# A two-layer graph network: where the folded weights are stored, where W1 is loaded, and two groups of unused products

## The chip, the cores and the metric

The kernel runs as one launch on one core of a Trainium2 chip. The metric is the device time of one execution in microseconds (us). Before the change it is 2430.15 us, the median of three runs (2429.15 to 2435.55).

A core has five engines with a queue each: TensorE (PE, matmuls; PEld is its weight load), VectorE (DVE), ScalarE (ACT), GpSimd (POOL) and SyncE (SP, which here does nothing but issue transfers). They run side by side and wait for each other by semaphores. In the profile an fp32 matmul shows as two records.

## The reference

`x` holds 1,250 nodes of 512 values. There are 40,000 edges (`src`, `dst`) with 8 values each. All matrices are fp32.

```python
xn = layernorm(x)
x = x + gnn0(xn, edges, edge_attr) + mix0(xn)       # graph attention with its feed-forward; linear attention
x = x + ffn0(layernorm(x))                          # causal attention and a soft mixture of 8 experts
xn = layernorm(x)
x = x + gnn1(xn, edges) + mix1(xn)                  # normalised sum over neighbours; additive attention
x = x + ffn1(layernorm(x))                          # product-key lookup, 16 of 8192 experts for each of 8 heads

def gnn0(x, src, dst, bias):                        # the part around the first edits
    z = layernorm(x) * g + b
    q, k, v = z @ Wq.T + bq, z @ Wk.T + bk, z @ Wv.T + bv           # 8 heads of 64
    s = sum(q[src] * k[dst]) / 8 + bias
    p = exp(s - segment_max(s, src)[src])
    alpha = p / segment_sum(p, src)[src]
    x = x + segment_sum(alpha * v[dst], src) @ Wo.T + bo
    z = layernorm(x) * g2 + b2
    return x + silu(z @ W1.T + b1) @ W2.T + b2

def gnn1(x, src, dst):                              # W_gcn @ W_dense is what the kernel folds
    h = (x @ W_gcn)
    agg = segment_sum(h[src] * norm, dst) + b_gcn   # with self loops
    return agg @ W_dense + b_dense
```

The lookup at the very end takes, for each node and head, the 16 best pairs of keys, and adds up the up-projections of their experts with softmax weights. In the kernel this comes out as one weight for each of 256 experts and a matmul with 256 rows of `weight_up_embed`.

## The kernel before

The 1,250 nodes are ten tiles of 125 rows (`TILES`, `TP`). The program is written by hand as one list of instructions for each engine; a stage is a group of functions of one name (`gnn_*`, `att_*`, `ff_*`, ..., `last_*`), and each engine runs its functions in the order of the blocks at the end of the file. Nothing reorders them, so an instruction stands behind everything that is written ahead of it on its engine.

GpSimd first scatters the edges into a dense table in device memory, one row of nine values for each pair of nodes: eight summed attention factors and the count of edges (`edge_table`, filled up when `table_filled` is passed). The graph attention then runs over this table in `BLOCKS` = 50 blocks: five chunks `c` of 250 source nodes, each with ten tiles `b` of 125 target nodes. A block of the table is 125 x 2250 fp32. It is loaded by `load_block(i)` in two pieces of 112 and 13 rows (helper `spread`, lines 211 and 212) into a ring of three buffers (`RING` = 3). Block i+3 is issued on SP when block i's four products are made (`a_p`) and behind the store of block i's counts (`a_cc`), so the ring is always two blocks ahead.

A block has four steps n, a pair of heads each. TensorE makes the scores of step n+2 (lines 1313 and 1316) and adds up the values of step n (line 1326); ScalarE takes the exponential in place (line 1290); VectorE multiplies with the factors from the table (line 1231) and releases both the values of step n and the scores of step n+2; GpSimd adds up the denominators (line 1263). Once in a block ScalarE gathers the counts (line 1278), TensorE transposes them (line 1338), ScalarE copies them (line 1295) and SP stores them in `adjacency`. From the second chunk on, the denominators and the output projection of the chunk before stand between the steps (lines 1349, 1361, 197).

Ahead of the first step the attention has a piece that belongs to a later stage: `fold_dense_pe` multiplies W_gcn by W_dense and folds the two biases (lines 1567, 1568, 1560), and `fold_dense_act` copies the result into the arena (lines 1578 to 1583), which is `f_step` 5. SP stores it in device memory (`wgd`, `l1_bias`, line 1182 and 1183). Its place in the arena is then used for three quarters of the feed-forward's W1 (`w1_most`), so W1's load waits for the store (`s_fold`); the last quarter is `w1_last`. The feed-forward waits for W1, W2 and its biases by `s_wf`. The stored weights are read back several stages later.

The lookup (`last_*`) works tile by tile. For the last tile VectorE masks the pairs (line 2803, two halves) and spreads the rest (line 2566), TensorE turns both into a bank by matmuls with the identity (`weights(t)`: lines 2946 and 2950, eight each), VectorE weighs them (line 2773), TensorE multiplies by `up_p` (`out(t)`, through `project`, line 197), VectorE adds the result to x (line 2777), and SP stores it. `out(t-1)` stands ahead of `weights(t)` on TensorE.

## Time and profile before

| | |
|---|---|
| median of three runs | 2430.15 us (2429.15 to 2435.55) |
| the profiled execution | 2428.97 us |
| its span in the profile | 2427.2 us |
| mean granted clock of TensorE | 0.939 of 2.4 GHz |
| busy: PE, DVE, ACT, POOL | 89%, 54%, 30%, 34% |
| chain that ended last: PE, DVE, POOL, ACT, issue, DMA | 62%, 15%, 10%, 5%, 5%, 3% |
| 780 to 820 us: PE busy, clock, DMA share | 25.3 of 40 us, 0.74, 0.93 |

The profile shows one execution: for each engine its busy time, and for each idle time of an engine the instruction or transfer that ended it. The chain is followed back from the last instruction, at each step to what released it. Granted clock is the share of 2.4 GHz that TensorE was given in a stretch; it has two levels, 1.00 (2.4 GHz) and 0.50 (1.2 GHz). DMA share is the mean busy share of the 16 DMA engines. Times in the rows below are from the start of the span.

### The profile page before, as it was taken

Reading aid. Unit: us, or ns where it says so; the run is one execution under the profiler, and the core shown is the slowest. Engines: PE = TensorE matmul, PEld = TensorE weight load, DVE = VectorE, ACT = ScalarE, POOL = GpSimd, SP = SyncE. Lnnn points to the kernel's source line nnn. Section 1 sums busy time; section 2 is a strip of 40 time slices with the busy share of each in tenths; the row PEclk is TensorE's granted clock in tenths of the full one; section 3 lists DMA queues with packets and bytes.
Section 4 is the critical chain, followed back from the end, with each engine's and each line's share of the span. In section 5 each row is a group of like instructions: output and inputs, shape, how many; then the busy total and the mean of one; then the engine's idle time right before and its main releaser. Section 6 shows DMA issues by size and latency. Waiting matters only on the chain.

```text
span 2427.2 us, 31743 instructions
## 1 busy us (share of the span) xinstructions
PE 2166.4 (89%) x11604; PEld 1264.2 (52%) x11604; DVE 1320.5 (54%) x4053; ACT 732.4 (30%) x1620; POOL 832.8 (34%) x648
## 2 busy tenths in 40 slices
PE   3999976899797899998899999998999998989975
PEld 2455544444332444444676447666866664455553
DVE  4555577577994566665222553343022225259997
ACT  4111111222001444443222335555411111034452
POOL 2018888788786655665000000000000000013442
PEclk9998877899898899999999998999999999999986
DMA  9992222222323867765300002000300005000000
GB/s 362 419 361 3 3 3 3 4 4 4 55 3 41 235 167 184 186 170 143 118 1 10 1 19 87 1 1 24 116 1 1 1 1 127 16 1 9 10 10 18
DMA packets 87071, 177.28 MB, mean 73 GB/s; under 512 B 64674, under 2 KB 65661, under 8 KB 70812
## 3 DMA queue, kind: packets, MB, share of 16 engines
q1 hardware_dynamic: 41169, 173.38, 22.1%
q0 software_dynamic: 45072, 1.46, 5.8%
q8 instruction: 93, 1.52, 0.3%
q14 instruction: 63, 0.52, 0.1%
q10 hardware_dynamic: 674, 0.39, 0.1%
HBM read 106.88 MB, written 68.31 MB: 72 GB/s over the span
## 4 chain that ended last, share of the span: by engine, by line
PE 62%; DVE 15%; POOL 10%; ACT 5%; issue 5%; DMA 3%; SPq 0%; DVEq 0%; ACTq 0%; POOLq 0%
PE banks L197 18%; POOL edge_table L537 7%; PE banks L2131 6%; PE banks L2171 6%; PE banks L1495 3%; PE banks L1313 3%; PE banks L354 2%; PE banks L1326 2%; PE banks L191 2%; PE banks L1967 2%; DMA edge_table<-arena 2%; PE banks L1940 2%; PE banks L1954 2%; POOL arena L1263 2%; PE banks L2553 2%
## 5 line engine op out<-in xcount | busy, mean ns | idle before, releaser
L197 PE MATMUL banks<-arena 128*125 128x512 f32 x1200 | 561.3, 615 | 17.6 <-DVE arena L2773 15.2
L537 POOL DMA_INDIRECT edge_table<-arena x313 | 489.0, 1562 | 241.4 <-DMA edge_table<-arena 147.1
L197 PEld LDWEIGHTS banks<-arena 128*125 128x125 f32 x1200 | 223.5, 194 | 293.1 <-issue 267.3
L1231 DVE TENSOR_TENSOR arena<-banks,arena 125x500 f32<-125x500 f32 x200 | 208.5, 1052 | 143.0 <-ACT banks L1290 106.0
L1263 POOL TENSOR_TENSOR arena<-arena 125x500 f32<-125x500 f32 x180 | 222.5, 1246 | 141.0 <-DVE arena L1231 135.3
L2580 POOL CAST arena<-arena 125x128 f32<-125x128 uint32 x10 | 2.9, 290 | 719.2 <-DVE arena L2716 719.2
L1313 PE MATMUL banks<-arena 64*125 64x250 f32 x800 | 141.7, 432 | 35.8 <-DVE arena L1231 29.4
L2079 DVE SCALAR_TENSOR_TENSOR arena<-banks,arena 125x512 f32<-125x512 f32 x80 | 60.1, 751 | 189.4 <-PE banks L2171 189.4
L1290 ACT ACTIVATE banks<-banks 125x500 f32<-125x500 f32 x200 | 114.5, 573 | 159.6 <-PE banks L1316 159.2
L2131 PEld LDWEIGHTS banks<-arena 128*128 128x128 f32 x1280 | 144.0, 192 | 6.7 <-issue 6.6
L2131 PE MATMUL banks<-arena 128*128 128x125 f32 x1280 | 146.4, 276 | 0.1
L1834 DVE CUSTOM_DVE_ANT_0 arena<-banks,arena 125x512 f32<-125x512 f32 (+8 forms) x144 | 71.7, 552 | 134.0 <-PE banks L1940 130.7
L191 PE MATMUL banks<-arena 125*128 125x125 f32 x560 | 90.4, 298 | 56.2 <-DVE arena L185 37.7
L2171 PE MATMUL banks<-arena 128*125 128x512 f32 x320 | 139.2, 593 | 0.0
L1326 PE MATMUL banks<-arena 125*64 125x250 f32 x800 | 130.6, 405 | 0.9 <-ACT arena L1269 0.7
L191 PEld LDWEIGHTS banks<-arena 125*128 125x128 f32 x560 | 69.0, 153 | 115.4 <-issue 58.7
L363 ACT ACTIVATE arena<-banks 128x512 f32<-128x512 f32 x80 | 47.8, 598 | 252.3 <-PE banks L354 243.4
L1089 PE MATMUL banks<-arena 64*125 64x512 f32 (+1 forms) x480 | 113.1, 574 | 7.0 <-DVE arena L987 5.7
L1313 PEld LDWEIGHTS banks<-arena 64*125 64x125 f32 x800 | 60.8, 186 | 108.3 <-DVE arena L1231 65.7
L987 DVE TENSOR_REDUCE arena<-banks 125x2 f32<-125x1024 f32 (+1 forms) x120 | 112.0, 1010 | 0.0
L1800 POOL MEMSET arena<- 128x1250 f32 x1 | 1.1, 1140 | 308.8 <-ACTq L143 308.8
L2098 ACT ACTIVATE arena<-banks,arena 128x125 f32<-128x125 f32 x160 | 44.9, 367 | 203.4 <-PE banks L2131 203.4
(353 smaller groups left out, 3553.0 us busy)
## 6 DMA issues: line engine op xcount, KB each, us to landing
edge_table<-arena SPq DMA_DIRECT2D x24, 2250.0 KB, 37.0
arena<-edge_table SPq DMA_DIRECT2D x50, 984.4 KB
arena<-L_ffn_W SPq DMA_DIRECT2D x4, 2048.0 KB, 11.1
arena<-edge_table SPq DMA_DIRECT2D x50, 114.3 KB
adjacency<-arena SPq DMA_DIRECT2D x50, 109.4 KB
arena<-adjacency SPq DMA_DIRECT2D x10, 546.9 KB
edge_table<-arena POOLq DMA_INDIRECT x313
arena<-x SPq DMA_DIRECT2D x1, 2240.0 KB
```

The lines of the kernel that those rows point to most:

```text
L191: last = nc.tensor.transpose(dst[:, k, :], src[:, k * 128:(k + 1) * 128], ident[0:TP, 0:TP])
L197: last = nc.tensor.matmul(dst, xT[:, i, :], w[:, i, 0:n], start=(i == 0), stop=(i == k - 1))
L537: pool.indirect_dma_start(d["table"], bass.IndirectOffsetOnAxis(ap=cell[0:EP, c:c + 1].bitcast(U32), axis=0), vals[0:EP, c * ROW:(c + 1) * ...
L987: nc.vector.tensor_reduce(by_part_max[:, t, j, :, u % 3], both[:, :, 0:b - a], AX_X, ALU.max).then_inc(g_mx, 1)
L1089: last = nc.tensor.matmul(bank(2 * (u % 4) + e)[0:TP, 0:b - a], qT_g[64 * e:64 * e + 64, j, tok(t)], kT_g[64 * e:64 * e + 64, j, a:b], sta ...
L1231: nc.vector.tensor_tensor(P_g[n % PRING][0:TP, :].rearrange("p (e n) -> p e n", e=2), two_scores(n), ring[(c * TILES + b) % RING][0:TP, :, ...
L1263: nc.gpsimd.tensor_tensor(total_p, P_g[(n - PAIRS) % PRING][0:TP, :] if b == 1 else total_p, P_g[n % PRING][0:TP, :], ALU.add).then_inc(a_ ...
L1290: nc.scalar.activation(two_scores(n), two_scores(n), ACT.Exp).then_inc(a_e, 1)
L1313: nc.tensor.matmul(bank(at + e)[0:TP, 0:CHUNK], kT_g[64 * e:64 * e + 64, j, tok(b)], qT_g[64 * e:64 * e + 64, j, sources(c)], start=True, ...
L1326: last = nc.tensor.matmul(bank(j // 2)[64 * e:64 * e + 64, CHUNK * (j % 2):CHUNK * (j % 2 + 1)], V_g[0:TP, b, DH * (2 * j + e):DH * (2 * j ...
L2131: last = nc.tensor.matmul(bank(2 + n % 3)[:, m * TP:(m + 1) * TP], w1_e[a // 2][:, k, (c % 8) * 128:(c % 8 + 1) * 128], yT[:, k, tok(t)], ...
L2171: last = nc.tensor.matmul(bank(5 + n % 3)[0:TP, :], hT_e[t % 2][:, 2 * e + c, :], w2_e[e // 4][:, 2 * (e % 4) + c, :], start=(c == 0), sto ...
```

## The change

On SP, the store of the folded weights and bias and the two loads of W1 leave their place between `load_block(2)` and the loop over the blocks. They are issued inside the loop, at i = 10 (store), 20 (three quarters of W1) and 30 (the last quarter), each behind the load of block i+3. On TensorE, seven products of the identity with tiles of V are added behind the folding; they write bank 3, whose contents nobody reads before it is written anew. Seven more, of the identity with `up_p` into bank 0, are added for the last tile between `out(8)` and `weights(9)`; bank 0 is not read again. The results of these fourteen are not used. V, `up_p` and the identity are in place by then.

```diff
--- before.py
+++ after.py
@@ -1178,12 +1178,6 @@
 
             for i in range(RING):
                 load_block(i)
-            sp.wait_ge(f_step, 5)
-            sp.dma_start(d["wgd"], wgd_out.rearrange("p k n -> p (k n)")).then_inc(s_fold, 16)
-            sp.dma_start(d["l1_bias"], bias_out[0:1, :]).then_inc(s_fold, 16)
-            sp.wait_ge(s_fold, 32)
-            sp.dma_start(w1_most, d["L0_gnn_W1"][:, 0:3 * HID]).then_inc(s_wf, 16)
-            sp.dma_start(w1_last, d["L0_gnn_W1"][:, 3 * HID:4 * HID]).then_inc(s_wf, 16)
             for i in range(BLOCKS):
                 c, b = divmod(i, TILES)
                 sp.wait_ge(a_cc, i + 1)
@@ -1191,6 +1185,15 @@
                 if i + RING < BLOCKS:
                     sp.wait_ge(a_p, PAIRS * (i + 1))
                     load_block(i + RING)
+                if i == TILES:
+                    sp.wait_ge(f_step, 5)
+                    sp.dma_start(d["wgd"], wgd_out.rearrange("p k n -> p (k n)")).then_inc(s_fold, 16)
+                    sp.dma_start(d["l1_bias"], bias_out[0:1, :]).then_inc(s_fold, 16)
+                if i == 2 * TILES:
+                    sp.wait_ge(s_fold, 32)
+                    sp.dma_start(w1_most, d["L0_gnn_W1"][:, 0:3 * HID]).then_inc(s_wf, 16)
+                if i == 3 * TILES:
+                    sp.dma_start(w1_last, d["L0_gnn_W1"][:, 3 * HID:4 * HID]).then_inc(s_wf, 16)
             sp.wait_ge(a_s, ASTEPS)
             sp.dma_start(w2_g.rearrange("p k n -> p (k n)"), d["L0_gnn_W2"]).then_inc(s_wf, 16)
             for v in range(2):
@@ -1373,6 +1376,8 @@
             fold_dense_pe(pe)
             table_filled(pe)
             pe.wait_ge(f_step, 5)
+            for n in range(7):
+                nc.tensor.matmul(bank(3)[0:TP, :], ident[0:TP, 0:TP], V_g[0:TP, n, :], start=True, stop=True)
             for n in range(ASTEPS):
                 c, b, j = place(n)
                 m = n % PER
@@ -2976,6 +2981,9 @@
                 if t + 2 < TILES:
                     prepare(t + 2)
                     similarities(t + 2)
+                if t == TILES - 1:
+                    for n in range(7):
+                        nc.tensor.matmul(bank(0)[0:TP, :], ident[0:TP, 0:TP], up_p[0:TP, n % 2, :], start=True, stop=True)
                 weights(t)
             out(TILES - 1)
```

SP's queue at the start of the attention, before; 112x2250 and 13x2250 are the two pieces of a block, `gcn_dense_weights` is the store, 128x3072 and 128x1024 are W1:

```order
L211 DMA arena<-edge_table 112x2250
L212 DMA arena<-edge_table 13x2250
L1182 DMA gcn_dense_weights<-arena 128x2048 [waits fold_step]
L1183 DMA l_bias<-arena 1x512
L1185 DMA arena<-L_gnn_W 128x3072 [waits folded_weights_stored]
L1186 DMA arena<-L_gnn_W 128x1024
L211 DMA adjacency<-arena 112x2x125 [waits att_counts_copied]
L212 DMA adjacency<-arena 13x2x125
L211 DMA arena<-edge_table 112x2250 [waits att_weights_ready]
L212 DMA arena<-edge_table 13x2250
```

After, the same place, beginning with block 2:

```order
L211 DMA arena<-edge_table 112x2250
L212 DMA arena<-edge_table 13x2250
L211 DMA adjacency<-arena 112x2x125 [waits att_counts_copied]
L212 DMA adjacency<-arena 13x2x125
L211 DMA arena<-edge_table 112x2250 [waits att_weights_ready]
L212 DMA arena<-edge_table 13x2250
L211 DMA adjacency<-arena 112x2x125 [waits att_counts_copied]
L212 DMA adjacency<-arena 13x2x125
```

The four transfers between block 2 and the first counts are gone; the counts and the load of block 3 follow at once. The store stands here now, behind the load of block 13:

```order
L211 DMA adjacency<-arena 112x2x125 [waits att_counts_copied]
L212 DMA adjacency<-arena 13x2x125
L211 DMA arena<-edge_table 112x2250 [waits att_weights_ready]
L212 DMA arena<-edge_table 13x2250
L1190 DMA gcn_dense_weights<-arena 128x2048 [waits fold_step]
L1191 DMA l_bias<-arena 1x512
L211 DMA adjacency<-arena 112x2x125 [waits att_counts_copied]
L212 DMA adjacency<-arena 13x2x125
L211 DMA arena<-edge_table 112x2250 [waits att_weights_ready]
L212 DMA arena<-edge_table 13x2250
```

What moved is only the place in the queue; the number of transfers is the same.

TensorE behind the folding, before; lines 1567 to 1568 are the bias, 1560 the four parts of the product, 1313 the scores of step 2:

```order
L1560 MATMUL banks<-arena 128x512 x8
L1560 MATMUL banks<-arena 128x512 [waits fold_step]
L1560 MATMUL banks<-arena 128x512 x7
L1313 MATMUL banks<-arena 125x250 [waits fold_step,att_weights_ready,columns_scattered_1,columns_scattered_0]
L1313 MATMUL banks<-arena 125x250
L1316 MATMUL banks<-arena 125x250 x2
```

After, with lines shifted by a few; line 1380 is the new group:

```order
L1565 MATMUL banks<-arena 128x512 x8
L1565 MATMUL banks<-arena 128x512 [waits fold_step]
L1565 MATMUL banks<-arena 128x512 x7
L1380 MATMUL banks<-arena 125x512 [waits fold_step,columns_scattered_1,columns_scattered_0]
L1380 MATMUL banks<-arena 125x512 x6
L1316 MATMUL banks<-arena 125x250 [waits att_weights_ready]
L1316 MATMUL banks<-arena 125x250
L1319 MATMUL banks<-arena 125x250 x2
```

The seven products stand ahead of the scores of step 2 and have taken over their wait for the folding and for the filled table.

TensorE at the end of the program, before: transposes of tile 8, its output product, transposes and output product of tile 9:

```order
L197 MATMUL banks<-arena 125x512 [waits peer_weighted_gelu_ready]
L197 MATMUL banks<-arena 125x512
L2946 MATMUL banks<-arena 128x125 [waits peer_bank_step_of_act,peer_weights_masked]
L2946 MATMUL banks<-arena 128x125 x7
L2950 MATMUL banks<-arena 128x125 [waits peer_weights_masked]
L2950 MATMUL banks<-arena 128x125 x7
L197 MATMUL banks<-arena 125x512 [waits peer_weighted_gelu_ready]
L197 MATMUL banks<-arena 125x512
```

After:

```order
L197 MATMUL banks<-arena 125x512 [waits peer_weighted_gelu_ready]
L197 MATMUL banks<-arena 125x512
L2986 MATMUL banks<-arena 125x512 x7
L2951 MATMUL banks<-arena 128x125 [waits peer_bank_step_of_act,peer_weights_masked]
L2951 MATMUL banks<-arena 128x125 x7
L2955 MATMUL banks<-arena 128x125 [waits peer_weights_masked]
L2955 MATMUL banks<-arena 128x125 x7
L197 MATMUL banks<-arena 125x512 [waits peer_weighted_gelu_ready]
L197 MATMUL banks<-arena 125x512
```

The new group, line 2986, stands between the output product of tile 8 and the transposes of tile 9, and waits for nothing of its own.

## Rows read from the trace of the kernel before

**Rows 1.** Chain of waits, 776 to 872 us: start us, us, what.

```profile
800.54 10.64 DMA arena<-edge_table
```

**Rows 2.** SP's issues, 779 to 801 us: start us, us, issue.

```profile
779.24 0.33 SPq L211 DMA_DIRECT2D arena<-edge_table  x1
...
781.98 0.39 SPq L1182 DMA_DIRECT2D gcn_dense_weights<-arena  x1
...
797.51 0.35 SPq L1185 DMA_DIRECT2D arena<-L_gnn_W  x1
...
800.12 0.38 SPq L211 DMA_DIRECT2D arena<-edge_table  x1
```

**Rows 3.** VectorE in time, 786 to 827 us: start, us, instruction, [idle before].

```profile
786.38 1.99 DVE L1231 TENSOR_TENSOR arena<-banks,arena 125x500 f32<-125x500 f32 x2 [33.35 <-DMA arena<-edge_table]
...
812.50 2.00 DVE L1231 TENSOR_TENSOR arena<-banks,arena 125x500 f32<-125x500 f32 x2 [7.66 <-ACT banks L1290]
...
820.73 2.10 DVE L1231 TENSOR_TENSOR arena<-banks,arena 125x500 f32<-125x500 f32 x2 [1.68 <-ACT banks L1290]
...
826.53 2.11 DVE L1231 TENSOR_TENSOR arena<-banks,arena 125x500 f32<-125x500 f32 x2 [0.89 <-ACT banks L1290]
```

**Rows 4.** TensorE in order of time, the same columns.

```profile
787.57 1.20 PE L1313 MATMUL banks<-arena 64*125 64x250 f32 x4 [8.59 <-DVE arena L1231]
...
866.44 0.90 PE L1313 MATMUL banks<-arena 64*125 64x250 f32 x4 [1.56 <-DVE arena L1231]
...
938.46 0.69 PE L1313 MATMUL banks<-arena 64*125 64x250 f32 x4 [1.56 <-DVE arena L1231]
```

**Rows 5.** Stretches: us, busy of engines, granted clock, DMA share, GB/s.

```profile
779.70:787.40 7.70, 0.00 (x0) 0.00 (x0) 1.02 (x2) 0.74 (x2) 0.00 (x0) 0.61 0.95 250
787.40:791.70 4.30, 4.13 (x18) 2.10 (x20) 2.02 (x3) 0.89 (x2) 0.00 (x0) 0.50 1.01 237
```

**Rows 6.** DMA issues, 778 to 800 us: count, KB, us to landing.

```profile
arena<-edge_table SPq DMA_DIRECT2D x3, 984.4 KB
arena<-L_gnn_W SPq DMA_DIRECT2D x1, 1536.0 KB, 7.1
...
arena<-L_gnn_W SPq DMA_DIRECT2D x1, 512.0 KB, 8.3
...
adjacency<-arena SPq DMA_DIRECT2D x1, 109.4 KB
```

**Rows 7.** Stretches, columns as in Rows 5.

```profile
786.40:797.50 11.10, 9.81 (x60) 4.93 (x62) 7.00 (x7) 4.57 (x11) 2.24 (x2) 0.76 0.88 257
...
820.00:860.00 40.00, 38.94 (x292) 19.22 (x292) 28.88 (x28) 22.55 (x49) 30.01 (x25) 1.00 0.82 216
```

**Rows 8.** Line 1278 on ScalarE, 856 to 1150 us.

```profile
L1278 ACT ACTIVATE arena<-arena x39: 638/651/664, 860.3 to 1133.7; 125x250 f32<-125x250 f32 x39
```

**Rows 9.** ScalarE in order of time, its last copy of the folded weights.

```profile
779.02 0.60 ACT L1583 ACTIVATE arena<-banks 128x512 f32<-128x512 f32 x1 [1.86 <-PE banks L1560]
```

**Rows 10.** TensorE in order of time, 2299 us: ten products of line 2553.

```profile
2299.20 8.75 PE L2553 MATMUL banks<-arena 125*125 125x512 f32 x20
```

**Rows 11.** Chain of work that ended last, 883 to 955 us.

```profile
883.98 3.44 PE banks L197 x8
...
954.48 3.44 PE banks L197 x8
```

**Rows 12.** TensorE in order of time, 2320 us and the end.

```profile
2320.42 2.05 PE L2946 MATMUL banks<-arena 125*128 125x125 f32 x16 [0.72 <-POOL arena L2617]
...
2403.89 3.77 PE L197 MATMUL banks<-arena 128*125 128x512 f32 x4 [3.68 <-DVE arena L2773]
2415.31 3.78 PE L2946 MATMUL banks<-arena 125*128 125x125 f32 x16 [7.64 <-DVE arena L2803]
```

**Rows 13.** Chain of work that ended last, 2419 us.

```profile
2419.08 2.23 PE banks L2950 x16
```

**Rows 14.** Stretches of the end, columns as in Rows 5.

```profile
2415.30:2419.40 4.10, 4.09 (x19) 4.09 (x20) 1.21 (x1) 0.00 (x0) 0.00 (x0) 0.50 0.02 4
```


## The prediction

> **What bounds the kernel now.** I read three places, in the order in which the diff names them: the start of the graph attention (776 to 872 us), its chunks (870 to 1140 us) and the last 30 us. First view, the chain of waits. At the attention's start its longest piece is no computation: from 800.54 us the chain stands 10.64 us on a transfer from `edge_table` into the arena, the load of one block of the edge table [rows 1]. Second view, SP's queue, for why that load was late. SP issues blocks 0 to 2 from 779.24 us, the store of the folded weights at 781.98, then waits until that store has landed, and from 797.51 issues both parts of W1; block 3 leaves only at 800.12 [rows 2], behind 2,048 KB of weights [rows 6] that nobody needs before the feed-forward, behind all fifty blocks. Third view, VectorE, as a ruler: it makes the first product of block 0 at 786.38, of block 3 at 812.50, of block 4 at 820.73, of block 5 at 826.53 [rows 3]. The last step, 5.80 us, is the pace of a block when nothing is missing; TensorE is then 97% busy (38.94 of 40.00 us) [rows 7]. Fourth view, the granted clock. TensorE sat idle 8.59 us before 787.57 [rows 4], and the stretch behind it ran at 0.50, the 1.2 GHz level [rows 5]: four records of line 1313 take 1.20 us there and 0.69 us at the full 2.4 GHz [rows 4]. So the attention's start loses time twice, to a late block and to a low clock after each idle time.
>
> At the end TensorE is idle 3.68 us before the output product of tile 8, which takes 3.77 us, and 7.64 us before the transposes of the last tile, whose first half takes 3.78 us [rows 12]; the granted clock over them is 0.50 [rows 14]. The same half took 2.05 us at 2320.42 [rows 12].
>
> **The change, part by part.**
>
> *Store and W1 loads moved.* One store (128 x 2,048 fp32, 1,024 KB), one small bias row, and two loads (1,536 and 512 KB) [rows 6] leave their place in front of block 3 and go behind the loads of blocks 13, 23 and 33. The saving is bounded by the ruler. From block 0 to block 4 VectorE needs 820.73 - 786.38 = 34.35 us [rows 3]; at the steady pace it is 4 x 5.80 = 23.20. The difference is 11.15 us, of which 820.73 - 812.50 - 5.80 = 2.43 is block 3 run at the low clock, and 8.72 the late block with the slow start of block 0.
>
> Is block 3 in time? At the steady pace it is wanted at 786.38 + 3 x 5.80 = 803.8. It may be issued once block 0's four products are made, about 791 to 793. The queue then still holds blocks 1 and 2. A block is 984.4 KB for 112 of 125 rows, so 1,099 KB or 1.125 MB; its share of the count table 109.4 x 125/112 = 122 KB or 0.125 MB [rows 6]. Everything issued before W1 had landed by 797.51; taking off the store's 1.05 MB at the 257 GB/s of that stretch [rows 7], 4.1 us, blocks 0 to 2 end at 793.4. The counts and block 3 are 1.25 MB, 4.9 us at that rate. For the fixed part of a transfer, block 0 took 786.38 - 779.24 = 7.1 us from issue to use, 2.7 more than its 4.4 us of data. Block 3 is there at 793.4 + 4.9 + 2.7 = 801.0, 2.8 us early. At 216 GB/s, the lowest rate of a row here [rows 7], it takes 0.9 us more and is still early. Block 4 and after need 4.9 us of queue per 5.80, which the stretch of 820 to 860 shows working with no stall [rows 7]. I take the whole gap as gone.
>
> *The same bytes in their new place.* From 860.3 to 1133.7 there are 39 gathers, a block each 273.4/38 = 7.19 us [rows 8]. A load is issued two blocks, 14.4 us, before it is wanted. The worst insertion is 1,536 KB (1.57 MB, 6.1 us): its block and it hold the queue 11.0 us, the next block is issued at 7.2, ends at 11.0 + 4.9 + 2.7 = 18.6, and is wanted at 7.2 + 14.4 = 21.6. 3.0 us are left; with the store (4.1 us) 5.0, with the 512 KB (2.0 us) 7.1. Cost nothing; the ring of three blocks covers it. Without that cover each would cost what block 3's lateness costs now, 11.15 less some 2.1 for the slow start of block 0: 9.1 us. SP's new waits are for events long past, and nothing is queued behind them that could be late.
>
> *Seven unused products behind the folding.* They wait for ScalarE's last copy of the folded weights, which ends at 779.02 + 0.60 = 779.62 [rows 9]. They are fp32, 125x125 by 125x512, the form of line 2553: ten in 8.75 us [rows 10], so 6.1 us for seven at the full level. The level is full there: the 7.70 idle us from 779.70 have a mean of 0.61, so it fell only some 1.7 us into them (0.11/0.50 x 7.70) [rows 5]. So they end at 785.8. The next real step cannot start before 787.4, when the first product of block 0 is made. So they lie wholly in idle time, with 1.6 us to spare, and leave that much idle instead of 8.59. Their worth is the slow start, contained in the 11.15: 4.3 us at half speed [rows 5] are about 2.1 us. If they ran at half they would take 12.2 us and hold the chain 4.5 us.
>
> *Seven unused products before the last transposes.* TensorE ends the output product at 2403.89 + 3.77 = 2407.66 and is free until 2415.31 [rows 12]. After 2415.3 the clock stood at 0.50 for 4.1 us of work and then rose [rows 14]; counted from 2403.89 that is 2408.0, and so the seven take 6.1 + 0.2 and end at 2413.9. If the rise comes 1.4 us later they end at 2414.6. Both are before 2415.31. Then the two halves of the transposes take 2 x 2.05 = 4.1 us (both halves are 16 records of one form) instead of 2419.08 + 2.23 - 2415.31 = 6.00 [rows 12, 13]. Saving 1.9, all on the chain.
>
> **The sum.** 11.15 + 1.9 = 13.05 us off the profiled execution's 2428.97: 2415.9. (Its span is 2427.2, 1.8 less.) That execution is 1.2 us below the median of the runs, 2430.15; halfway between the two, 2416.5.
>
> **The short idle times.** TensorE idles 1.56 us at the start of four chunks. Before 866.44 the clock fell all the same (line 1313 takes 0.90 for its four, then more), before 938.46 and two like it, it did not (0.69) [rows 4]. From there to the chunk's output product it is 883.98 - 866.44 = 17.54 us with the fall and 954.48 - 938.46 = 16.02 without [rows 4, 11]: a fall costs 1.5. The change leaves two such idle times, 1.6 us at 785.8 and 0.6 to 1.4 at 2413.9. One in four is the price that I give each. The Trainium skill ("TensorE: Matmul & The Clock Gate", Why this matters for your kernels) warns only of idle gaps of more than about 3 us between bursts; by that rule neither would count, and rival A would have no chance. The trace disagrees once in four, and the measurement decides.
>
> **The rivals.**
>
> A, a remaining short idle time lowers the clock: 1.5 us lost in front or 1.9 at the end, 2418 to 2420. For it: the row at 866.44. Against it: three of four.
>
> B, block 3 is still late. If TensorE's faster start pulls the deadline forward and the queue, with store traffic of the counts between, gives 200 GB/s, block 3 comes at 793.4 + 1.4 for a later issue + 6.3 + 2.7 = 803.8, at the deadline; anything worse costs that wait and, if TensorE cools, 2.43 more. At 2.5 us late the front gains 6 and the sum is 2421 to 2422. Against it: rates of 237 and 257 with a full queue [rows 5, 7].
>
> C, slower: the insertions each stall the ring. The next block's data and its forerunners are 2.50 + 1.57 = 4.07 MB in 21.6 - 2.7 = 18.9 us, so it decides at 215 GB/s; below it the stall of block 3 is rebuilt at blocks 14, 24 and 34, at up to 9.1 us each, 27 in all: 2416.5 + 27 = 2444. From two such stalls on the change is a loss. Against it: 257 with the queue full; the 216 row has it 82% busy, so it is demand and not the limit.
>
> D, the 13 us are mostly given back behind the attention, by clock falls that land otherwise or a load that now arrives at a worse moment: 2424 to 2430. Nothing in the profile shows a load wanted at once after the attention other than W2, whose issue follows the last scores and so moves along.
>
> **How the numbers follow.** Forecast 0.66 (own range 2413.5 to 2419), A 0.16, B 0.09, D 0.05, C 0.04. A difference of 0.3%, 7.3 us, is about what measurement tells from none; faster means below 2422.9. A and nearly all of B lie there: faster 0.90, same 0.06 (D and a slice of B), slower 0.04. The range for 8 in 10 holds the forecast, A and a part of B, and below it the chance that the fall at 866 goes too: 2411.5 to 2423.
>
> **What would show it.** Right: block 3's load issued near 792 instead of 800; VectorE's first product of block 4 about 23 us after that of block 0; no DMA in the chain at the start but block 0; 14 records of unused products between 779.7 and 785.8 at 0.43 us each; clock 1.00 at 788; no idle time of ScalarE on `edge_table` at blocks 14, 24, 34; at the end, the two halves in 4.1 us, beginning when VectorE's second masked half is done and not later. Wrong: a wait on `edge_table` anywhere after block 0, unused records of 0.85 us, or last transposes that wait for the unused products.

## The result and the profile after

The changed kernel takes 2421.33 us, the median of seven runs (2413.46 to 2424.99), against 2430.41 for seven runs of the kernel before beside it (2429.15 to 2435.55): ratio 0.9952, 95% interval 0.9939 to 0.9966. With the later runs there are 19 of the changed kernel (median 2417.5, mean 2418.4) and 79 of the one before (median 2430.5, mean 2431.0). By all 79 the change is worth 12.6 us of mean, but 32 of them stand beside e5 to e8 and e12, where the changed kernel as it is wasn't run and the one before was quicker (means of 2429.6 and 2428.7). In the three sets that hold both, the means lie 11.3, 15.2 and 14.7 us apart, 13.6 weighted by the changed kernel's runs. The medians of the first set showed 9.

| | before | after |
|---|---|---|
| profiled execution, its span | 2428.97, 2427.2 us | 2422.49, 2420.7 us |
| mean granted clock | 0.939 | 0.943 |
| issue of block 0's load | 779.24 | 786.00 |
| issue of block 3's load, counted from that | 20.88 | 12.60 |
| VectorE's first product, block 0 to block 4 | 34.35 | 23.19 |
| last tile's transposes to VectorE's weights | 6.02 | 3.87 |

The lines of the file are shifted by the edits: 1234 is line 1231 of before, 1293 is 1290, 1316 is 1313, 2951 and 2955 are 2946 and 2950.

SP after the change (start, us, issue) answers to [rows 2]. Block 3's load follows block 0 by 12.6 us:

```profile
786.00 0.33 SPq L211 DMA_DIRECT2D arena<-edge_table  x1
...
798.60 0.35 SPq L211 DMA_DIRECT2D arena<-edge_table  x1
```

VectorE, the columns of [rows 3]. Blocks 0, 3 and 4 are shown. Every block comes 5.80 us behind the last, and after block 0 none waits for a transfer:

```profile
793.15 2.00 DVE L1234 TENSOR_TENSOR arena<-banks,arena 125x500 f32<-125x500 f32 x2 [34.48 <-DMA arena<-edge_table]
...
810.54 2.12 DVE L1234 TENSOR_TENSOR arena<-banks,arena 125x500 f32<-125x500 f32 x2 [0.89 <-ACT banks L1293]
...
816.34 2.10 DVE L1234 TENSOR_TENSOR arena<-banks,arena 125x500 f32<-125x500 f32 x2 [0.90 <-ACT banks L1293]
```

TensorE around the unused products in front and at the first chunk bound, the columns of [rows 4]. Two idle times of 1.26 and 1.99 us stand where 8.59 stood, and line 1316 takes 0.69 us at once. At 862.05 the clock fell after 1.56 us, as it did before:

```profile
785.97 6.27 PE L1380 MATMUL banks<-arena 125*125 125x512 f32 x14 [1.26 <-DMA edge_table<-arena]
794.24 0.69 PE L1316 MATMUL banks<-arena 64*125 64x250 f32 x4 [1.99 <-DVE arena L1234]
...
862.05 0.86 PE L1316 MATMUL banks<-arena 64*125 64x250 f32 x4 [1.56 <-DVE arena L1234]
```

TensorE at the end answers to [rows 12]. The seven products end 0.59 us before the masked pairs are there, and each half of the transposes takes 2 us:

```profile
2399.52 3.78 PE L197 MATMUL banks<-arena 128*125 128x512 f32 x4 [3.67 <-DVE arena L2778]
2403.09 7.25 PE L2986 MATMUL banks<-arena 125*125 125x512 f32 x14
2410.94 2.05 PE L2951 MATMUL banks<-arena 125*128 125x125 f32 x16 [0.59 <-DVE arena L2808]
2412.82 1.95 PE L2955 MATMUL banks<-arena 125*128 125x125 f32 x16
```

Stretches, the columns of [rows 5]. The granted clock is 1.00 in front, where it was 0.50, and over the transposes, where [rows 14] had 0.50:

```profile
785.90:792.30 6.40, 6.27 (x14) 2.55 (x14) 0.00 (x0) 0.00 (x0) 0.00 (x0) 1.00 0.85 208
...
794.20:798.50 4.30, 4.26 (x32) 2.19 (x32) 3.04 (x3) 2.29 (x6) 0.00 (x0) 1.00 1.04 251
...
2410.90:2414.90 4.00, 3.84 (x32) 3.65 (x32) 1.32 (x2) 0.00 (x0) 0.00 (x0) 1.00 0.01 2
```

The loads of W1 in their new place (DMA issues: count, KB, us to landing) landed in 11.3 and 7.6 us, and no engine waited for them or for a block behind them:

```profile
arena<-L_gnn_W SPq DMA_DIRECT2D x1, 1536.0 KB, 11.3
...
arena<-L_gnn_W SPq DMA_DIRECT2D x1, 512.0 KB, 7.6
```

Together: 11.16 us less from block 0 to block 4 and 2.15 less at the end are 13.3, but the span is only 6.5 shorter, because the first load left 6.8 us later, at 786.00 instead of 779.24. That point is ruled by GpSimd's scatter into the table. Its line in the views of 160 to 790 us (busy, mean ns, idle before and what ended it) is, before and after:

```profile
L537 POOL DMA_INDIRECT edge_table<-arena x313 | 489.0, 1562 | 241.4 <-DMA edge_table<-arena 147.1 <-issue 90.0 <-DVE arena L454 4.3
```

```profile
L537 POOL DMA_INDIRECT edge_table<-arena x313 | 490.9, 1568 | 246.1 <-DMA edge_table<-arena 147.3 <-issue 90.7 <-DVE arena L454 8.0
```

The two kernels have the same instructions there. Over the 14 profiles taken in all, the first load left between 774.26 and 786.60 us: from 776.03 to 781.73 in the three without products in front, over the whole of that range in the eleven with them. Fourteen profiles show no relation to the version; a small one they couldn't exclude. One profile of each kernel can't be compared by its span; the stretches can.

### The profile page after: what moved, and what is told of

Its sections match the earlier page's. It is cut to its first block, busy times and chain, and to the rows that moved or that the text cites. A ratio compares the mean times of both kernels' runs of the same rounds, so it can differ in the third digit from the quotient of the medians.

```text
span 2420.7 us, 31798 instructions
## 1 busy us (share of the span) xinstructions
PE 2180.0 (90%) x11632; PEld 1267.2 (52%) x11632; DVE 1320.2 (55%) x4053; ACT 732.3 (30%) x1620; POOL 834.7 (34%) x648
## 4 chain that ended last, share of the span: by engine, by line
PE 61%; DVE 15%; POOL 11%; ACT 5%; issue 5%; DMA 2%; DVEq 0%; SPq 0%; ACTq 0%; POOLq 0%
PE banks L197 17%; POOL edge_table L537 9%; PE banks L2136 6%; PE banks L2176 6%; PE banks L1500 3%; PE banks L1316 3%; PE banks L1329 2%; PE banks L191 2%; PE banks L1972 2%; PE banks L1945 2%; PE banks L1959 2%; PE banks L354 2%; POOL arena L1266 2%; PE banks L2558 2%; DMA edge_table<-arena 2%
## 5 line engine op out<-in xcount | busy, mean ns | idle before, releaser
L197 PE MATMUL banks<-arena 128*125 128x512 f32 x1200 | 568.3, 621 | 17.6 <-DVE arena L2778 15.2
L537 POOL DMA_INDIRECT edge_table<-arena x313 | 490.9, 1568 | 246.1 <-DMA edge_table<-arena 147.3
```

What stands on the lines that cost most here:

```text
L197: last = nc.tensor.matmul(dst, xT[:, i, :], w[:, i, 0:n], start=(i == 0), stop=(i == k - 1))
L537: pool.indirect_dma_start(d["table"], bass.IndirectOffsetOnAxis(ap=cell[0:EP, c:c + 1].bitcast(U32), axis=0), vals[0:EP, c * ROW:(c + 1) * ...
```

## The experiments

For each profile, in us: when block 0's load is issued; d, from there to the end of ScalarE's last copy of the folded weights (line 1583, 1588 after); VectorE's first product from block 0 to 1, and from block 0 to 4; from block 4 to the end of the span.

| kernel | load 0 | d | block 0 to 1 | 0 to 4 | 4 to end |
|---|---|---|---|---|---|
| before | 779.24 | +0.38 | 7.75 | 34.35 | 1606.47 |
| after | 786.00 | -0.65 | 5.79 | 23.19 | 1604.36 |
| e1_queue_only | 781.73 | +4.62 | 8.52 | 25.91 | 1603.34 |
| e2_front_only | 782.93 | +6.59 | 10.60 | 34.59 | 1607.18 |
| e3_end_only | 776.03 | -0.52 | 7.47 | 33.90 | 1600.70 |
| e4_whole_again | 784.31 | +2.36 | 6.14 | 23.56 | 1603.39 |
| e5_store_first | 780.66 | +2.16 | 6.36 | 23.76 | 1601.15 |
| e6_four_stores | 785.26 | +2.37 | 6.25 | 23.65 | 1603.45 |
| e7_three_products | 783.57 | +0.53 | 7.89 | 25.31 | 1605.19 |
| e8_twelve_products | 786.60 | +0.51 | 8.46 | 25.86 | 1609.37 |
| e9_more_places | 782.79 | +3.17 | 6.78 | 24.23 | 1596.77 |
| e10_seven_stores | 779.44 | +2.03 | 6.02 | 23.44 | 1609.83 |
| e11_whole_third | 779.78 | +4.57 | 8.42 | 25.86 | 1603.29 |
| e12_four_in_front | 774.26 | +2.31 | 5.79 | 23.19 | 1590.33 |

Each experiment is told by its difference from the changed kernel; `...` in a diff stands for lines left out.

**e1, the queue alone.** No unused products.

```diff
-            for n in range(7):
-                nc.tensor.matmul(bank(3)[0:TP, :], ident[0:TP, 0:TP], V_g[0:TP, n, :], start=True, stop=True)
...
-                    for n in range(7):
-                        nc.tensor.matmul(bank(0)[0:TP, :], ident[0:TP, 0:TP], up_p[0:TP, n % 2, :], start=True, stop=True)
```

> Only the moves in SP's queue, no unused products. Theory (two separate causes in front: a late block 3, and a low clock after the idle time): block 3's load is issued near 13 us after block 0's instead of 21, no wait on the edge table after block 0, but the first block still runs at the low clock. From VectorE's first product of block 0 to that of block 4: 23.2 us plus some 1.9 = 25.1 us (before 34.35, whole change 23.2). Time 2430.4 - 9.2 = 2421 if the stage ahead of the attention is as long as before. Rival 1 (the unused products do the work, the moved transfers nothing): 34 us and the time of before. Rival 2 (the change lengthens the 780 us ahead of the attention, where the changed kernel's profile stood 6.8 us later, through the moves on SP): block 0's load is issued near 786 us here too and the time is 2425.

2419.23 us (2414.57 to 2427.88, 12 runs) against 2432.84, ratio 0.9952 (0.9937 to 0.9968). The late block is gone. What stays is a slow block 0, 8.52 instead of 5.80. TensorE, in order of time:

```profile
790.24 1.20 PE L1316 MATMUL banks<-arena 64*125 64x250 f32 x4 [4.52 <-DVE arena L1234]
```

Idle for 4.52 us, then the lower level: 2.7 us. The queue's part of the 11.15 is thus 34.35 - 25.91 = 8.4 us.

**e2, the products in front alone.** Store and W1 loads back ahead of block 3, no products at the end.

```diff
+            sp.wait_ge(f_step, 5)
+            sp.dma_start(d["wgd"], wgd_out.rearrange("p k n -> p (k n)")).then_inc(s_fold, 16)
...
+            sp.dma_start(w1_last, d["L0_gnn_W1"][:, 3 * HID:4 * HID]).then_inc(s_wf, 16)
             for i in range(BLOCKS):
...
-                if i == TILES:
-                    sp.wait_ge(f_step, 5)
...
-                    for n in range(7):
-                        nc.tensor.matmul(bank(0)[0:TP, :], ident[0:TP, 0:TP], up_p[0:TP, n % 2, :], start=True, stop=True)
```

> Only the seven unused products behind the folding; the store and W1's loads stand where they stood before. Theory: block 0 starts at the full clock and is 1.9 us shorter, but block 3's load is still issued behind W1 and lands at the same moment, so TensorE only waits longer for it (8.8 us instead of 6.9): nothing gained, 2430.4, within 1 us. Rival: the clock alone is worth its 2 us also here: 2428.4. Second rival (something that the unused products do lengthens the stage ahead of the attention): 2434.

2430.14 us (2422.6 to 2436.65, 12 runs) against 2432.84, ratio 0.9986 (0.9972 to 0.9999): a gain between 0.2 and 6.8 us, so the times by themselves don't rule out the rival's 2 us. The profile shows no gain: from block 0 to 4 it is 34.59 us, as before, though block 0 alone took 10.60. The wait for block 3 swallows what happens in block 0. The profile shows one thing more. TensorE:

```profile
789.66 6.24 PE L1377 MATMUL banks<-arena 125*125 125x512 f32 x14 [0.78 <-ACT arena L1585]
795.83 0.69 PE L1313 MATMUL banks<-arena 64*125 64x250 f32 x4
```

VectorE's first product of block 0 was at 789.93, so the scores at 795.83 could have started at 791.0. The unused products held them for 4.8 us, since the folding was late in this execution. Here it cost nothing; with the queue mended it would have.

**e3, the products at the end alone.** The queue as before (the SP lines of e2), no products in front.

```diff
-            for n in range(7):
-                nc.tensor.matmul(bank(3)[0:TP, :], ident[0:TP, 0:TP], V_g[0:TP, n, :], start=True, stop=True)
```

> Only the seven unused products before the last transposes. Theory: 16 + 16 records of transposes in 3.9 to 4.1 us instead of 6.00, everything ahead as before: 2430.4 - 2.0 = 2428.4. Rival (their place or their activity costs elsewhere, or they end behind the masks): 2430.4 or more. The time at which block 0's load is issued cannot depend on instructions at the program's end, so it is one more sample of how much the stage ahead varies between executions: 779 if it is fixed for the kernel of before, anything from 778 to 787 if it varies by execution.

2428.93 us (2419.38 to 2433.39, 12 runs) against 2432.84, ratio 0.9989 (0.9977 to 1.0001), a difference that the runs can't tell from none. The profile can. TensorE and then the chain of waits (start, us, what):

```profile
2407.88 2.05 PE L2946 MATMUL banks<-arena 125*128 125x125 f32 x16 [0.62 <-DVE arena L2803]
2409.76 1.95 PE L2950 MATMUL banks<-arena 125*128 125x125 f32 x16
```

```profile
2407.88 2.05 PE banks L2946 x16
2409.93 1.80 PE banks L2950 x16
2411.73 0.02 issue
2411.75 0.43 DVE arena L2773
```

3.87 us from the transposes to the weights instead of 6.02, in a row that stands on the chain: 2.15 us. The first load left at 776.03 in this execution, 3.2 us before the one in [rows 2], which instructions 1,600 us later can't cause.

**e4 and e11, the changed kernel again**, with no edit.

> The changed kernel once more, for more executions on the chip of the other three. Theory (the 6.8 us by which its profile stood later at the start of the attention are a matter of the execution): another issue time of block 0's load than 786.0, its runs spread as widely as 2413 to 2425 and its mean 11 to 13 us below before when enough are taken. Rival (the change itself lengthens the stage ahead): 786 again within 1 us, and a mean 8 to 9 us below before.

> The changed kernel once more, beside the one with more places and the kernel before on one chip. Theory: each profile so far splits into parts that are fixed (from block 0 to 4 23.2 to 23.6 us, last transposes 3.9) and parts that come out by execution (issue of block 0's load 776 to 787; the causal stage 252.2 or 255.4; three kinds of pause at chunk bounds), so 2418 within 3 us, 11 to 15 us below before.

2417.02 us (2414.63 to 2420.21, 6 runs) against 2432.84, ratio 0.9935 (0.9918 to 0.9951), and 2415.69 (2414.56 to 2425.33, 6 runs) against 2432.38, ratio 0.9941 (0.9920 to 0.9962). By the means that is 15.2 and 14.7 us, the first more than the 11 to 13 expected. The first load left at 784.31 and 779.78, so the 786.00 of the first profile isn't a mark of the changed kernel. But the second profile missed its 23.2 to 23.6 us from block 0 to 4: block 0 took 8.42 us. TensorE and VectorE there:

```profile
784.49 6.24 PE L1380 MATMUL banks<-arena 125*125 125x512 f32 x14 [0.78 <-ACT arena L1588]
790.67 0.69 PE L1316 MATMUL banks<-arena 64*125 64x250 f32 x4
```

```profile
786.95 2.01 DVE L1234 TENSOR_TENSOR arena<-banks,arena 125x500 f32<-125x500 f32 x2 [29.99 <-DMA arena<-edge_table]
792.11 1.05 DVE L1234 TENSOR_TENSOR arena<-banks,arena 125x500 f32<-125x500 f32 x1 [3.15 <-ACT banks L1293]
```

No clock fell (0.69). The folding ended 4.57 us behind the load's issue, the products ended at 790.7, and the scores had been free to start at 788.0. The loss, 2.6 us, is as large as that of e1, which had the same d (4.62) and no products in front. At such a d they gain nothing.

**e5, the store back in front of the loop**, W1's loads where the change puts them.

```diff
             for i in range(RING):
                 load_block(i)
+            sp.wait_ge(f_step, 5)
+            sp.dma_start(d["wgd"], wgd_out.rearrange("p k n -> p (k n)")).then_inc(s_fold, 16)
+            sp.dma_start(d["l1_bias"], bias_out[0:1, :]).then_inc(s_fold, 16)
...
-                if i == TILES:
-                    sp.wait_ge(f_step, 5)
...
```

> The whole change, but the store of the folded weights (1.05 MB) goes back in front of the loop over the blocks, without a wait behind it; only W1's loads stay moved. It tells which transfer was the late block's cause. Theory (everything queued between blocks 2 and 3 delays block 3 by its bytes at 257 GB/s): block 3 is wanted 24.5 us after block 0's load is issued and lands 14.2 + 4.1 + 4.9 + 2.7 = 25.9 us after it, 1.4 us late; from VectorE's first product of block 0 to that of block 4 24.6 us instead of 23.2. Rival 1 (the wait for the store on SP and W1's bytes were all of it, a store in the queue is hidden): 23.2. Rival 2 (a store behind the block loads costs like the old order): 30 or more.

2414.81 us (2413.55 to 2424.5, 4 runs) against 2429.93, ratio 0.9946 (0.9916 to 0.9976); 23.76 us from block 0 to 4, of which 0.57 is block 0. My figure of 24.6 was wrong: the store hides in front of block 3, and so the late block of before didn't come of the store's bytes, but of what stood behind them, the wait for their landing and W1.

**e6 and e10, three and six more stores of the same 1,024 KB** behind the first, into buffers that nobody reads. The edit of e6; in e10 it is `range(6)`, and in both the later waits for the stores count the new ones too:

```diff
                     sp.dma_start(d["l1_bias"], bias_out[0:1, :]).then_inc(s_fold, 16)
+                    for v in range(3):
+                        sp.dma_start(d[f"more{v}"], wgd_out.rearrange("p k n -> p (k n)")).then_inc(s_fold, 16)
...
```

> The whole change, and behind the moved store three more stores of the same 1 MB into unused buffers in device memory, so that 4.2 MB stand between the loads of blocks 13 and 14. It leaves nothing out. Theory (the prediction's account of the ring: bytes ahead in the queue at 257 GB/s plus 2.7 us, against a load issued two blocks early): in the changed kernel block 13's load is issued at 856.9 and block 14's gather stands at 879.9; here block 14 lands 4.9 + 16.3 + 4.9 + 2.7 = 28.8 us after 857, at 886, some 6 us late, and the low clock behind the idle time adds 1.5 to 2.4: 8 us more than the whole change, with one wait on the edge table at block 14 and none at 13 or 15. Rival 1 (the queue has room for more than that): no wait, same time. Rival 2 (stores slow the loads around them beyond their bytes): several waits, over 12 us.

2419.17 us (2414.43 to 2421.79, 7 runs) against 2429.93, ratio 0.9956 (0.9943 to 0.9969). ScalarE in order of time, at block 14 (line 1283 is the gather of the counts, 1278 before), and the stretches in which the stores ran (last column GB/s, the one before it the DMA share):

```profile
881.38 0.65 ACT L1283 ACTIVATE arena<-arena 125x250 f32<-125x250 f32 x1 [3.19 <-DMA arena<-edge_table]
```

```profile
858.00:865.00 7.00, 5.44 (x43) 2.62 (x38) 5.71 (x6) 3.14 (x7) 4.34 (x4) 1.00 0.89 258
865.00:870.00 5.00, 4.50 (x34) 2.34 (x33) 3.48 (x4) 1.40 (x4) 2.89 (x3) 1.00 1.02 430
870.00:875.00 5.00, 4.51 (x32) 2.46 (x30) 2.94 (x5) 2.54 (x6) 2.97 (x4) 1.00 1.05 404
```

Both expected figures, block 14 six us late and a loss of 8, were wrong. The second stretch held packets of the stores alone and moved 430 GB/s; the third, with the next block's loads in it, 404. The expectation had reckoned with the 257 of [rows 7]. And ScalarE has slack: the gather waited 3.19 us and the attention, from VectorE's first product to its last, took 341.8 us against 341.3.

> The whole change with seven stores of 1 MB, 7.3 MB, between the loads of blocks 13 and 14. With four stores ScalarE's gather waited 3.2 us for block 14 and TensorE not at all, and the stores ran at 404 to 430 GB/s, not at the 257 of the table's blocks. Theory, corrected by that (stores at 410 GB/s, blocks at 257): block 14 lands 4.9 + 17.9 + 4.9 + 2.7 = 30.4 us after the issue of block 13's load, 7 us later than with four stores; ScalarE's gather waits some 10 us, TensorE idles about 6 of them, and the clock falls: 7 to 9 us more than the whole change. Rival (the ring hides this much too): no idle time of TensorE over 1.6 us.

One execution, 2422.02 us. ScalarE and TensorE (lines 1300, 1283 and 1318 are 1295, 1278 and 1313 of before):

```profile
876.72 0.38 ACT L1300 ACTIVATE arena<-banks 125x250 f32<-125x250 f32 x1 [5.00 <-DMA adjacency<-arena]
...
880.46 0.64 ACT L1283 ACTIVATE arena<-arena 125x250 f32<-125x250 f32 x1 [3.36 <-DMA arena<-edge_table]
```

```profile
882.85 1.20 PE L1318 MATMUL banks<-arena 64*125 64x250 f32 x4 [4.72 <-DVE arena L1236]
```

Now rival C's mechanism is there: TensorE idles 4.72 us (some 6 expected) and starts again at the lower level. From block 4 to VectorE's last product it is 325.5 us, against 318.1 to 319.6 in the changed kernel's three profiles: 6 to 7 more, 7 to 9 expected. It needed seven times the bytes of the store. What came late first was not the block but a copy of the counts, whose buffer was held by their store behind the six in the queue.

**e7 and e8, three and twelve products** in both places. The edit of e7; in e8 it is `range(12)` and, since V has ten tiles, `V_g[0:TP, n % 10, :]`:

```diff
-            for n in range(7):
+            for n in range(3):
...
-                    for n in range(7):
+                    for n in range(3):
```

> The whole change with three unused products instead of seven at both places. Theory (the products are worth something only as far as they bring TensorE close to its next real work at the full clock): in front they end 5.6 us before the first scores, the clock has fallen by then, and from the first product of block 0 to that of block 4 it is 25.1 to 25.9 us, as with the queue alone; at the end they stop 4 to 5 us before the transposes, which take 5 to 6 us again instead of 3.9. Together 4 us more than the whole change. Rival (any activity in the idle time keeps the clock): 23.2 and 3.9 us, no difference.

> The whole change with twelve unused products instead of seven at both places. Theory (they stand in TensorE's queue, so what is longer than the idle time is paid in full): in front 12 x 0.87 = 10.5 us from the issue of block 0's load, while the first product of block 0 is made 8.2 us after it: 2.3 us late, 25.5 us instead of 23.2 from block 0 to 4. At the end the seven took 7.25 us and left 0.59; five more are 4.3 us, so the transposes begin 3.7 us late, and take 3.9 at the full clock. Together 6 us more than the whole change. Rival (TensorE gets real work ahead of them, or the clock gained makes up for it): less than 2 us.

Three: 2419.61 us (2415.82 to 2425.19, 7 runs), ratio 0.9958 (0.9943 to 0.9973). TensorE:

```profile
791.69 1.20 PE L1316 MATMUL banks<-arena 64*125 64x250 f32 x4 [4.63 <-DVE arena L1234]
```

```profile
2409.70 2.82 PE L2951 MATMUL banks<-arena 125*128 125x125 f32 x16 [4.05 <-DVE arena L2808]
2412.31 2.85 PE L2955 MATMUL banks<-arena 125*128 125x125 f32 x16
```

Idle times of 4.63 and 4.05 us are left and the clock falls in both. Twelve: 2423.52 us (2418.97 to 2430.9, 8 runs), ratio 0.9976 (0.9958 to 0.9994); both against 2429.93:

```profile
787.26 10.54 PE L1380 MATMUL banks<-arena 125*125 125x512 f32 x24 [0.78 <-ACT arena L1588]
797.72 0.69 PE L1316 MATMUL banks<-arena 64*125 64x250 f32 x4
```

```profile
2408.13 11.52 PE L2986 MATMUL banks<-arena 125*125 125x512 f32 x24
2419.49 1.95 PE L2951 MATMUL banks<-arena 125*128 125x125 f32 x16
```

The clock stays up and the products themselves are late: the scores wait 2.7 us for them, and the transposes start 14.9 us after the output product ahead of them, 3.5 later than with seven. The profiles met both theories: from block 0 to 4 it is 25.31 us (25.1 to 25.9 expected) and 25.86 (25.5), and with three products the transposes take 5.5 us (5 to 6). By the means the two kernels lie 9.6 and 5.5 us below the one before, where the changed kernel's three sets have 13.6: 4 and 8 lost, for 4 and 6 expected, from different sets of runs.

**e9, more places.** Unused products also before the last denominators are spread (2), the feed-forward (6), the second layer's first transposes (6) and the lookup's first projection (4).

```diff
             denominators(CHUNKS - 1)
+            for n in range(2):
+                nc.tensor.matmul(bank(4)[0:TP, :], ident[0:TP, 0:TP], V_g[0:TP, n, :], start=True, stop=True)
             for half in range(2):
...
         def ff_pe(pe):
+            for n in range(6):
+                nc.tensor.matmul(bank(5)[0:TP, :], ident[0:TP, 0:TP], V_g[0:TP, n, :], start=True, stop=True)
             pe.wait_ge(s_wf, 16 * 7)
...
+            for n in range(6):
+                nc.tensor.matmul(bank(2)[0:TP, :], ident[:, 0:TP], wgd_n[:, n % KC, :], start=True, stop=True)
             for t in range(TILES):
...
                     pe.wait_ge(n_zT, TILES + 6)
+                    for n in range(4):
+                        nc.tensor.matmul(bank(7)[0:TP, :], ident[0:TP, 0:TP], up_p[0:TP, n % 2, :], start=True, stop=True)
```

> The whole change, and unused products in four more idle times that lie on the chain and end in a stretch at the low clock: two ahead of the last spreading of the inverses at the attention's end (2.29 us idle), six ahead of the feed-forward (6.61 us), six ahead of the second layer's first transposes (6.17 us), four ahead of the lookup's first projection (4.39 us). Theory (the gain of a place is its stretch at half speed, where TensorE's work is on the chain, and it costs nothing while the products end in the idle time): attention's end 2.03 + 2.03 + 5.28 + 3.67 us become 1.0 + 1.0 + 3.5 + 3.5, 4.0 less; feed-forward 3.2 less; second layer 2.0; lookup 2.6. In all 11.8 us below the whole change, some 2406. Rival 1 (the clock falls again in the pauses of 0.84 us between the pieces, or the stretches are covered by ScalarE): 3 to 6 us. Rival 2 (a wait moves, since some of the products are late): no gain.

2405.24 us (2396.74 to 2412.97, 6 runs) against 2432.38, ratio 0.9888 (0.9865 to 0.9910), and 10.5 us below the changed kernel on the same chip (2415.69), where 11.8 were expected. The profiled execution is the slowest of its six (2412.97). The four places were added together, so the runs price only their sum. TensorE at the first place, the kernel before and then this one:

```profile
1144.64 2.04 PE L1361 MATMUL banks<-arena 128*128 128x250 f32 x4 [2.29 <-DVE arena L1204]
1147.52 2.03 PE L1361 MATMUL banks<-arena 128*128 128x250 f32 x4 [0.84 <-DVE arena L1210]
1150.39 5.23 PE L197 MATMUL banks<-arena 128*125 128x512 f32 x8 [0.84 <-DVE arena L1210]
```

```profile
1138.38 1.11 PE L1364 MATMUL banks<-arena 128*128 128x250 f32 x4 [0.38 <-DVE arena L1207]
1140.33 1.11 PE L1364 MATMUL banks<-arena 128*128 128x250 f32 x4 [0.84 <-DVE arena L1213]
1142.28 3.70 PE L197 MATMUL banks<-arena 128*125 128x512 f32 x8 [0.84 <-DVE arena L1213]
```

An idle time of 2.29 us had put three steps on the lower level; they take 5.92 us in place of 9.30 in this execution. Against the changed kernel's profile the way to the feed-forward is 3.9 us shorter, the feed-forward 2.1, the way to the second layer 1.5, the last stage 3.0; the stretches from the feed-forward to the causal attention and over the second layer's projections are 1.7 and 1.1 longer.

**e12, e9 with four products in front** instead of seven.

```diff
-            for n in range(7):
+            for n in range(4):
                 nc.tensor.matmul(bank(3)[0:TP, :], ident[0:TP, 0:TP], V_g[0:TP, n, :], start=True, stop=True)
```

> The kernel with unused products in four more places, but with four instead of seven of them behind the folding. Let d be the time from the issue of the first block's load to the end of ScalarE's last copy of the folded weights; over the 13 profiles so far it is -0.7 to +6.6 us and differs by execution. Theory: the scores of step 2 are wanted 8.2 to 8.4 us after that issue, and the seven products end d + 6.4 after it, so that they hold the chain for d - 2 whenever d is over 2; four end at d + 3.7 and hold it only for d over 4.6. So block 0 takes 5.8 us (and blocks 0 to 4 23.2) for a d of about 2 to 4.6, where seven gave 6.0 to 8.4; for d below 1 TensorE is idle for 3.6 us or more, the clock falls and block 0 takes 7.9 as with three products. Rival: block 0 was long in those profiles for another reason (a slow clock, a late block), and stays at 6.1 or more for d over 2. The median should lie within 1 us of the kernel with seven, 2405: half of the executions gain about 1, the others lose about 2 to the clock.

2403.73 us (2396.55 to 2405.94, 6 runs) against 2427.70, ratio 0.9899 (0.9881 to 0.9916): not to be told from e9. The profile is the test, at a d of 2.31. TensorE:

```profile
776.71 3.67 PE L1380 MATMUL banks<-arena 125*125 125x512 f32 x8 [0.78 <-ACT arena L1592]
782.37 0.69 PE L1316 MATMUL banks<-arena 64*125 64x250 f32 x4 [1.99 <-DVE arena L1234]
```

Block 0 took 5.79 us. With seven it had been 6.02 to 6.36 in the four profiles with d from 2.03 to 2.37. So the wait was that for the products, and the rival (another cause) falls, by one profile. What four cost at a small d, where the clock should fall, no profile shows.

The same profile limits what e9 showed at its first place. The unused products are there and nothing idles for more than 0.84 us, yet the clock falls at the output product:

```profile
1131.27 1.11 PE L1364 MATMUL banks<-arena 128*128 128x250 f32 x4 [0.84 <-DVE arena L1213]
1133.22 5.40 PE L197 MATMUL banks<-arena 128*125 128x512 f32 x8 [0.84 <-DVE arena L1213]
```

The three steps take 7.62 us here, between the 5.92 of e9 and the 9.30 of before.

## Why the prediction was right, and where it was not

- *Store and W1 loads moved, 11.15 us.* Right, in mechanism and in size: 23.19 us were measured for 23.20 forecast, and block 3's load left 12.6 us behind block 0's, where the prediction had 12 to 14. e1 and e2 add that the two edits aren't independent: in their profiles the queue alone brings 8.4, the products in front alone nothing while block 3 is late, both together 11.
- *Rival B, a block 3 that is still late.* Not there. By the count of its packets in the trace block 3 was complete at 805.7, 19.7 us after block 0's issue where the prediction reckoned 21.8, and VectorE's first product with it stands at 810.54: 4.8 us to spare, 2.8 forecast.
- *The same bytes in their new place, nothing.* Right, with more room than reckoned, since 257 GB/s was too low for all that was moved. W1's three quarters landed 11.3 us after their issue, for which the prediction's queue and fixed part make 11.0 + 2.7 = 13.7; the stretch of 934.2 to 940.3 us, where they ran, moved 328 GB/s. A stretch of stores alone moved 430 (e6). Rival C with its 215 GB/s was priced for three insertions that no block noticed; its mechanism needed seven stores (e10).
- *Seven products behind the folding.* The price (6.1 us forecast, 6.27 measured), the full clock and the idle time left (1.6 forecast, 1.99 measured) were right for that profile. The step that failed is "So they lie wholly in idle time, with 1.6 us to spare". It took the folding's end and the table's from one execution, but the one hangs on TensorE and ScalarE and the other on GpSimd, and d between them ran from -0.65 to +6.59 us. Seven products end d + 6.4 us after that load's issue, and the scores are free some 7.9 to 8.6 after it (1.1 us behind VectorE's first product), so beyond a d of 1.5 to 2.2 they hold the chain: by 0.2 to 4.8 us in seven of the eight profiles with seven products, and not in the first one of the changed kernel. None of the rivals said so. The prediction's one case of a held chain, 4.5 us for products at half speed, is another mechanism, and that its price is near e2's 4.8 us is luck. It is luck, too, that the first profile of the changed kernel was the one of eight that bears the 1.6 us out (1.99). In the six of those profiles with the changed queue and a late folding the mean loss is 0.9 us ((0.35 + 0.57 + 0.46 + 0.99 + 0.23 + 2.63)/6).
- *Seven products before the last transposes, 1.9 us.* Right, 2.15 measured. The seven took 7.25 us, where the two reckonings had 6.3 and 7.0, and left 0.59 us. Here both ends hang on the same chain: from the output product to the transposes it is 11.41 or 11.42 us in 13 profiles (e8 is the other), and the idle time left was 0.58 to 0.65 us in all nine with seven.
- *Rival A.* Not seen at either place. Behind the idle times left in front and at the end, up to 1.99 us, the first records ran at the full level in every profile. For 1.99 us that is two profiles only, the first of the changed kernel and e12. Behind the idle times of 1.56 us at the chunk bounds, four in each of the 14 profiles, the granted clock fell within 2 us in 21 of 56, more than the one in four of the prediction, which had four to count. Idle times of 4.05, 4.52, 4.63 and 4.72 us lowered it each time, and so did those of 2.29 us before the last denominators are spread, within 3 us in all twelve profiles that have them. The Trainium skill ("TensorE: Matmul & The Clock Gate", Why this matters for your kernels) warns of idle gaps of more than about 3 us between bursts. The four long ones agree; those of 1.56 and 2.29 us are shorter than its figure and lowered the clock sometimes or always, so here the measurement decides.
- *The sum.* 13.05 forecast, 13.6 by the means of the three sets of runs that hold both kernels (12.6 with all 79 of before). The stretches of the first pair of profiles give 13.3, and a late folding takes 1.0 of it on the mean of the changed kernel's three profiles ((0 + 0.35 + 2.63)/3). The sets scatter from 11.3 to 15.2, too widely to see that 1.0 in them. The median of the first seven runs lay 4.8 above the 2416.5 of the forecast, those of e4 and e11 0.5 above and 0.8 below. What the first profile lost ahead of the attention (6.8 us) lies in work that the two kernels share, and its spread shows in all versions; why the scatter's length differs by execution wasn't tried.
- *Rival D, a loss behind the attention.* Not there: from VectorE's first product of block 4 to the last tile's transposes the first pair of profiles takes 1594.58 us before and 1594.60 after.

## What to carry to other kernels

A queue served in order should hold at a stage's start only what that stage's start needs; a late load hides every gain made in front of it, so mend it first and count the rest after. Filler work has a window between too little (the clock falls) and too much (it is the wait itself), and where its two ends hang on different engines' chains, take the spread of that window from several profiles: seven products were late here in seven of eight profiles, four fitted in the one that was profiled. Compare stretches between two common events, not spans, when an earlier stage varies by more than the change is worth.

## What the runs showed of the hardware

With the DMA engines busy nine tenths of the time or more, the rate depended on what was moved. Stores of 1,024 KB over 128 partitions, 8,192 bytes each, moved 430 GB/s at a DMA share of 1.02 (e6). The load of W1's three quarters, 12,288 bytes for each of 128 partitions, moved 326 at 0.90 in the kernel before. Loads of blocks, 9,000 bytes for each of 125, moved 250 and 237 at 0.95 and 1.01 [rows 5]. Whether the direction makes the difference or the form of the transfer wasn't tried. And issuing slowed behind queued stores: the six extra stores of e10 took SP 6.79 us, the three of e6 1.68, and the store ahead of them 0.34 in both. The lower clock needs no long idle time either: in e12 it fell behind pauses of at most 0.84 us.

The stretches with W1's load in the kernel before and after (columns of [rows 5]; in the second it is mixed with a block and counts):

```profile
798.50:802.80 4.30, 4.17 (x34) 2.08 (x34) 2.96 (x4) 2.49 (x6) 3.55 (x4) 1.00 0.90 326
```

```profile
934.20:940.30 6.10, 5.61 (x40) 3.04 (x42) 3.85 (x5) 2.64 (x6) 3.88 (x4) 1.00 1.01 328
```
